# An attention and two-expert block on one core: gating and summing the last tiles elsewhere, TensorE products without a reader, and a third buffer of rows to be sorted

## The reference, cut to what matters

```python
mod = (silu(c) @ wmod).reshape(16, 6, 1, 256)     # sa, ca, ga, sb, cb, gb
ga, gb = sign * maximum(abs(.), 0.25)
h = layernorm(x) * (1 + ca) + sa                  # x: 16 batches x 256 tokens x 256
x = x + ga * attention(h)                         # 16 heads of 16, causal, low-rank q and kv
h = layernorm(x) * (1 + cb) + sb
# each token goes to one of two experts, by argmax of h @ Wg.T
out0 = gelu(h @ W0a.T + b0a) @ W0b.T + b0b
out1 = relu(h @ W1a.T + b1a) @ W1b.T + b1b
x = x + gb * where(expert == 0, out0, out1)
```

## Time and profile before

| | us |
|---|---|
| median of 3 runs | 574.53 (572.4 to 578.16) |
| the profiled execution: its time | 571.48 |
| its span | 569.7 |
| mean granted TensorE clock | 0.917 |
| busy: PE, PEld, DVE, ACT, POOL | 459.9, 364.0, 431.3, 293.4, 213.2 |

### The profile page before, as it was taken

One profiled execution on the slowest core, in us unless ns is written; L12 is line 12 of the kernel. 1 busy time (PEld: TensorE's weight loads), 2 busy tenths in 40 slices (PEclk: granted clock), 3 DMA queues, 4 the chain that ended last, 5 costly groups with the idle time before them and its releaser, 6 DMA issues.

```text
span 569.7 us, 11638 instructions
## 1 busy us (share of the span) xinstructions
PE 459.9 (81%) x4137; PEld 364.0 (64%) x4137; DVE 431.3 (76%) x987; ACT 293.4 (51%) x425; POOL 213.2 (37%) x233
## 2 busy tenths in 40 slices
PE   5627589889889889899889998898407999999950
PEld 4325467668668667667666777566306988888850
DVE  3657547798898898998888997785622799999960
ACT  1253157456466465465464674356204777677630
POOL 8422022323343343343242353213330044455475
PEclk9957679999999999999999999899656999999995
DMA  8596596596897898898899787723359514470111
GB/s 259 180 120 85 74 133 86 101 151 77 165 143 157 164 136 165 169 134 170 165 112 186 151 116 156 159 99 108 96 188 355 197 37 149 160 281 5 38 55 55
DMA packets 58793, 78.87 MB, mean 138 GB/s; under 512 B 6880, under 2 KB 47457, under 8 KB 58737
## 3 DMA queue, kind: packets, MB, share of 16 engines
q1 hardware_dynamic: 53632, 60.94, 57.9%
q0 software_dynamic: 4288, 16.80, 7.7%
q10 hardware_dynamic: 816, 0.39, 0.3%
HBM read 34.12 MB, written 18.96 MB: 93 GB/s over the span
## 4 chain that ended last, share of the span: by engine, by line
PE 35%; issue 27%; POOL 14%; DVE 10%; DMA 9%; ACT 2%; SPq 2%; POOLq 1%; ACTq 0%; DVEq 0%
DMA sorted_scratch<-comb,pos 5%; POOL out L1461 5%; PE ps_s L463 5%; PE ps_t L489 5%; POOL tile_rows L1454 5%; PE ps_o L506 4%; PE ps_s L443 3%; PE ps_t L443 3%; DVE mx L1110 2%; PE ps_o L507 1%; DVE z L988 1%; PE ps_c L410 1%; SPq L318 1%; DMA ks<-parts_k 1%; PE ps_a L524 1%
## 5 line engine op out<-in xcount | busy, mean ns | idle before, releaser
L1110 DVE TENSOR_REDUCE mx<-ps_s 128x2 f32<-128x512 f32 (+1 forms) x192 | 123.7, 684 | 38.6 <-PE ps_s L443 37.5
L867 ACT ACTIVATE p_all<-ps_t 128x1024 f32<-128x1024 f32 x93 | 95.1, 1023 | 98.4 <-PE ps_t L443 97.8
L463 PE MATMUL ps_s<-ks,qs 96*128 96x256 bf16 (+1 forms) x512 | 74.5, 255 | 37.2 <-issue 28.6
L463 PEld LDWEIGHTS ps_s<-ks,qs 96*128 96x128 bf16 x512 | 40.0, 101 | 54.1 <-issue 41.2
L489 PE MATMUL ps_t<-qs,ks 99*128 99x128 bf16 (+1 forms) x496 | 58.3, 251 | 4.6 <-DMA qs<-mx_rows 3.6
L443 PE MATMUL ps_s<-future_b,ident_b 128*128 128x256 bf16 (+1 forms) x192 | 61.8, 322 | 0.0
L1363 POOL TENSOR_TENSOR comb<-z,xs 128x512 f32<-128x512 f32 x16 | 20.4, 1276 | 102.8 <-DMA sorted_scratch<-comb,pos 62.2
L1454 POOL TENSOR_TENSOR tile_rows<-tile_rows 128x512 f32<-128x512 f32 x18 | 26.2, 1456 | 64.6 <-DVE tile_rows L1295 64.5
L489 PEld LDWEIGHTS ps_t<-qs,ks 99*128 99x128 bf16 x496 | 38.5, 99 | 15.0 <-issue 5.4
L1351 POOL TENSOR_TENSOR ln_rs<-ln_ve,neg_half 128x2 f32<-128x2 f32 x32 | 22.7, 711 | 66.8 <-DVE ln_ve L967 66.6
L410 PE MATMUL ps_s<-down_w,hid_hi 128*128 128x256 f32 x144 | 41.5, 288 | 4.6 <-DVE hid_lo L1275 4.6
(11 more groups left out here) (208 smaller groups left out, 1229.0 us busy)
## 6 DMA issues: line engine op xcount, KB each, us to landing
qs<-parts_q SPq DMA_DIRECT2D x96, 128.0 KB
ks<-parts_k SPq DMA_DIRECT2D x96, 128.0 KB
tile_rows<-sorted_scratch SPq DMA_DIRECT2D x9, 1026.0 KB, 9.7
rows<-mod_rows_scratch SPq DMA_DIRECT2D x16, 384.0 KB, 4.2
tile_rows<-sorted_scratch SPq DMA_DIRECT2D x9, 512.0 KB, 6.6
xs<-x SPq DMA_DIRECT2D x16, 256.0 KB, 6.0
comb<-mod_rows_scratch SPq DMA_DIRECT2D x32, 128.0 KB, 4.8
sorted_scratch<-wa SPq DMA_DIRECT2D x1, 1026.0 KB, 7.6
```

Source lines behind the costliest of these rows:

```text
L463: pe.matmul(ps_s[:, n * width:(n + 1) * width], qs[b.third][0:R, h, tile * P:(tile + 1) * P], ks[b.third][0:R, h, 0:width], start=n % a_ba ...
L867: act.activation((p0, p1)[tile][:, h0:h0 + n, :], scores_t(b, c)[:].rearrange("p (h s) -> p h s", h=n), ACT.Exp, scale=SCALE).then_inc(exp ...
L1110: dve.tensor_reduce(mx[:, tile, h0:h0 + n], ps_s[:, 512 * bank:512 * (bank + 1)].rearrange("p (h k) -> p h k", h=n), AX_X, ALU.max).then_i ...
```

## The change

There are three parts.

1. `comb`, `pos` and the semaphores `last_in` and `put` go from two buffers to three (index `b.third`, turns counted by `b.round`); the same four waits are now for the scatter of three batches before.
2. After the product that counts the first expert's rows (L687), TensorE makes 36 products of 512 bf16 columns into one half of `ps_s`. Nothing reads them. They wait for nothing, and `turn_tile(0)` stands behind them.
3. In the last turn of VectorE's loop (i = 8) the two `gate` operations of tile 7 stand right behind its `add_bias`, ahead of `hidden(8, 0)`, and no longer near the end of the turn. For tile 8 VectorE itself adds x1 after the gate, two more operations of 128x512, and GpSimd leaves out its two `finish_half`, so that `put_half` waits for VectorE's `last_ready`.

```diff
-        self.turn = n // 2
+        self.turn, self.round = n // 2, n // 3
-        pos = [sb(f"pos{i}", [P, TT], I32) for i in range(2)]
+        pos = [sb(f"pos{i}", [P, TT], I32) for i in range(3)]
-        comb = [early(f"comb{i}", [P, TT, ROW]) for i in range(2)]
+        comb = [early(f"comb{i}", [P, TT, ROW]) for i in range(3)]
+        WARM = 36
...
@@ SyncE, load_last_gate; place, add_attn and number_rows in the same way
-                wait(sp, put[b.pair], 32 * b.turn)
+                wait(sp, put[b.third], 32 * b.round)
...
-            for n in range(2):
-                sp.wait_ge(put[n], 16 * NB)
+            for n in range(3):
+                sp.wait_ge(put[n], 32 * ((NB - n + 2) // 3))
...
@@ TensorE
+            for n in range(WARM):
+                pe.matmul(ps_s[:, 512:1024], ident_b[:], future_b[:].unsqueeze(1).to_broadcast([P, 4, P]), start=True, stop=True)
             turn_tile(0)
...
@@ VectorE
             for i in range(NT):
                 add_bias(i - 1, 0)
                 add_bias(i - 1, 1)
+                if i == NT - 1:
+                    gate(i - 1, 0)
+                    gate(i - 1, 1)
                 hidden(i, 0)
...
-                gate(i - 1, 0)
-                gate(i - 1, 1)
+                if i < NT - 1:
+                    gate(i - 1, 0)
+                    gate(i - 1, 1)
                 target_rows(i)
             for q in range(2):
+                some = half_rows(NT - 1, q)
                 add_bias(NT - 1, q)
                 gate(NT - 1, q)
+                dve.wait_ge(y_gated, 2 * NT - 1 + q)
+                dve.tensor_tensor(some[:, :, 0:D], some[:, :, 0:D], some[:, :, D:2 * D], ALU.add).then_inc(last_ready, 1)
...
@@ GpSimd, put_half
-                pool.wait_ge(out_ready, 2 * i + q + 1)
+                if i < NT - 1:
+                    pool.wait_ge(out_ready, 2 * i + q + 1)
+                else:
+                    pool.wait_ge(last_ready, q + 1)
...
                 for q in range(2):
-                    finish_half(i, q)
+                    if i < NT - 1:
+                        finish_half(i, q)
                     put_half(i, q)
```

More of the change, by code:

```diff
@@ L223, in block_kernel @@
             "up_done gelu_done hid_ready hid_hi_ready hid_lo_ready down_part down_done".split())
[L224 removed]
+        y_ready, y_gated, out_ready, last_ready, row_of_ready = (sem(n) for n in "y_ready y_gated out_ready last_ready row_of_ready".split())
         g_in, rest_in, out_stored = ([sem(f"{n}{i}") for i in range(TILES)] for n in ("g_in", "rest_in", "out_stored"))
[L226 removed]
+        x_in, rows_in = (x_in0, x_in1), (rows_in0, rows_in1)
+        last_in, put = ([sem(f"{n}{i}") for i in range(3)] for n in ("last_in", "sorted"))
         q_in, k_in = (q_in0, q_in1), (k_in0, k_in1)
@@ L978, in second_stats @@
                     return
-                stats(b, 1, comb[b.pair][:, :, D:2 * D], x1_ready, b.n + 1)
+                stats(b, 1, comb[b.third][:, :, D:2 * D], x1_ready, b.n + 1)
             def normalise(b):
@@ L1036, in place @@
                 dve.wait_ge(offset_ready, b.n + 1)
-                wait(dve, put[b.pair], 32 * b.turn)
-                dve.tensor_tensor(pos[b.pair][:], BANK["RANK"][:, 0:TT], offset[:], ALU.add).then_inc(pos_ready, 1)
+                wait(dve, put[b.third], 32 * b.round)
+                dve.tensor_tensor(pos[b.third][:], BANK["RANK"][:, 0:TT], offset[:], ALU.add).then_inc(pos_ready, 1)
             def low_parts(some):
@@ L1357, in add_attn @@
                 pool.wait_ge(gated_ready, b.n + 1)
-                wait(pool, put[b.pair], 32 * b.turn)
+                wait(pool, put[b.third], 32 * b.round)
                 if b.n < 2:
@@ L1362, in add_attn @@
                 wait_alone(pool)
-                pool.tensor_tensor(comb[b.pair][:, :, D:2 * D], gated[:], xs[:, slots_of(b), :], ALU.add).then_inc(x1_ready, 1)
+                pool.tensor_tensor(comb[b.third][:, :, D:2 * D], gated[:], xs[:, slots_of(b), :], ALU.add).then_inc(x1_ready, 1)
             def number_rows(b):
@@ L1381, in put_rows @@
                 pool.wait_ge(number_ready, b.n + 1)
-                pool.wait_ge(last_in[b.pair], 32 * (b.turn + 1))
+                pool.wait_ge(last_in[b.third], 32 * (b.round + 1))
                 pool.wait_ge(x1_ready, b.n + 1)
                 for t in range(TT):
-                    pool.indirect_dma_start(sorted_dram, bass.IndirectOffsetOnAxis(ap=pos[b.pair][:, t:t + 1], axis=0),
-                                            comb[b.pair][:, t, :], None).then_inc(put[b.pair], 16)
+                    pool.indirect_dma_start(sorted_dram, bass.IndirectOffsetOnAxis(ap=pos[b.third][:, t:t + 1], axis=0),
+                                            comb[b.third][:, t, :], None).then_inc(put[b.third], 16)
             def h_low(b):
```

20 lines of the change are left out of this document (10 added, 10 removed).

## The result

The changed kernel took 580.50 us, median of 7 (577.84 to 583.40), against 576.04, median of 7 (572.40 to 578.16), for the kernel before. The ratio is 1.0089, 95% interval 1.0051 to 1.0127: slower by about 5 us, where I had forecast 6 us faster. The profiled execution of the changed kernel took 583.40 us with a span of 580.9, 11.2 more than the span before. That execution was the slowest of its seven, and the profiled one of before (571.48) was faster than all of its seven, so the two traces differ by 11 us where the medians differ by 4.5.

The account below looks back on a forecast made before the run. Usual first-stage steps were taken as bound by a ring of TensorE, SyncE's twelve issues and the transfers. End 3.6, products 0.9 and buffers 1.5 made 6.0 us off 574.53: 568.5 us, range 563.5 to 572.5.

Parts of the forecast that it names:

- The rival "slower": First-stage steps: VectorE running ahead lengthens TensorE's idle and the clock falls; up to 11 us slower, 585.6; chance 0.06.
- three buffers: First-stage steps: usual ones gain 0 as the stack's landing stays; two long ones give most of 1.5 us gained.
- The end: Last tiles: GpSimd loses two additions and the pauses behind them, gaining 3.6 us, bound 4.2; moved gates count 0.
- the pessimistic working: Last tiles: VectorE, with moved gates and two sums, is done by 557.1, before GpSimd reaches tile 8 at 557.57.
- The 36 products: Before the first tile: 10.8 us hidden under the load; faster transposes gain 0.9 us, 2.8 if the clock holds.
- 5.24 us after the work on the first tile had begun: First tile: when full clock returned; applied to the 36 products, it makes 12 slow and 24 fast.
- The rival that it holds: First tile: full clock lasts through the gap into up(0), giving 2.8 instead of 0.9 us, 566.6; chance 0.25.
- At most 8.9 of the 62.2 us reached another engine: First stage: of GpSimd's add_attn waits for scatters, only VectorE's 8.9 us wait was seen behind them.
- steps under 21 us: Sign in the changed profile that VectorE or GpSimd bounds the steps and the buffers are worth more than forecast.
- the buffers give nothing: First stage: the ring of stacks bounds every step, or earlier loads take the gain back; 570.0 to 572.0; chance 0.18.

Follow-up runs that it names:

- e1: Kernel before with only the third buffers of comb and pos, old end, without the 36 products: 587.39 us, ratio 1.0196.
- e3_wait_kept: Kernel before with only the third buffers, but add_attn still waits for the scatter of two batches before: 585.24 us, ratio 1.0167.
- e2: Kernel before with the new end and the 36 products, still two buffers: 571.01 us, ratio 0.9913.
- e12: Changed kernel plus 32 unused bytes behind pos and 10 unread products between the first tile's turning and its first products: 544.65 us, ratio 0.9467.
- e6: Changed kernel plus 32 unused bytes a partition behind the third pos, putting the stacks at a multiple of 256: 545.00 us, ratio 0.9443.
- e11: Changed kernel plus 160 unused bytes behind pos, putting the stacks 128 beyond a multiple of 256: 571.32 us, ratio 0.9926.
- e13: Kernel before plus 32 unused bytes behind the stacks, which stay while x, parts, rows and comb move: 576.33 us, ratio 1.0002.
- e15: Kernel before with the stacks moved 64 bytes to a multiple of 256 and everything behind them moved 512: 570.55 us, ratio 0.9905.
- e9: Kernel before plus 64 unused bytes behind pos, putting the stacks at a multiple of 256: 570.09 us, ratio 0.9903.
- e10: Kernel before plus 64 unused bytes behind pos, the new end and the 36 products, still two buffers: 563.38 us, ratio 0.9779.

## Why the prediction was wrong

**The sign and the size.** The forecast was 568.5 us with a range of 563.5 to 572.5; the result, 580.5, is outside on the other side. The rival that is slower had 0.06 of the chances. (The ratio of 1.0089 still lies within the 1% either way that had 0.43.)

**The step that failed** is the one on three buffers: "In usual steps what is late next is the landing of the stack, which doesn't move: 0." I had found the right bound, and took it as fixed. The landing moved by 0.25 us on average (15.74 to 15.99), because the new `pos` moved the stacks by 32 bytes. The idle of 1.5 to 2.1 us ahead of a step became 2.0 to 3.1, and the clock fell in eight of the twelve steps compared, not one. The term was +1.5 us with a lower bound of -2; alone it measured -11 (e1). In the early steps the idle grew by just what the landing did. Later it grew by some 0.5 us, and where the other half of that comes from stays open; e3_wait_kept has idles as long, so it isn't the scatter's wait.

**The rival "slower"** had the mechanism and its price: more idle at the start of a step, a fall of the clock, 1.95 us a fall (measured 1.8), up to 11 us. It had the wrong cause, VectorE running ahead, and I gave it 0.06 because that cause is weak. It is: e3_wait_kept takes it away and the falls stay. That it named the right sign is luck: the way to it was another. The rows that should have raised its chance whatever the cause were in the prediction: idles of 1.82 and 2.55 us with a fall behind them and of 2.14 without. Where nearly every step has such an idle, any of them may lose the clock; here landings a quarter of a us later went with falls in eight steps of twelve.

**The end** was worked out as 3.6 with a bound of 4.2. GpSimd's stretch is 4.2 us shorter in all, but that is no meeting of the bound. Tiles 7 and 8, which the sum is about, give 3.4: two issues took 1.36 and 1.00 beside VectorE's work, for 0.99 and 0.97, and the first addition 0.2 less. Another 0.8 come in tile 6, where issues of 1.41 and 1.37 us shrank to 0.97; the prediction had allowed 0.4 for one of them and counted 0. e2 has this part and the 36 products together at 5.0. VectorE's second sum was ready 0.43 us ahead of the first issue for tile 8, where the pessimistic working had left 0.47; but only the first sum is wanted by then, and it was 2.5 us early.

**The 36 products** gave 0.87 where 0.94 were worked out for the transposes, and the load landed 0.3 us later. They took 10.12 us where 10.8 were worked out. The "5.24 us after the work on the first tile had begun" counts from the first product; the transposes had begun 4.54 us earlier. The clock fell again in the standing for the split, as forecast. The rival that it holds (1.9 us more) was not this kernel; with the gap filled (e12) it is worth 1.7.

**The third buffers in themselves.** "At most 8.9 of the 62.2 us reached another engine" was right for this ring. It is a statement about the ring: with the stacks at a multiple of 256 the same wait decides, and the buffers are worth 19 us. The sign "steps under 21 us" for buffers that are worth more came in e6 (20.23). At the longer ring the buffers gave nothing (e11 against e2), which is the rival "the buffers give nothing": 570.0 to 572.0 us were forecast for it, and e11 took 571.32.

The best version by ratio, e6_aligned, is the changed kernel and one unused line: 545.0 us, ratio 0.9443, against 1.0089 without that line.

## What to carry to other kernels

An edit that allocates anything moves what is allocated behind it; ask which DMA destinations lie there, and look at the packets' durations before and after. Where transfers into SBUF bound a loop, try their destinations at multiples of 256 bytes in a partition before judging any other change. Here 32 bytes more made the changed kernel 6.4% faster, and the third buffers, which gained nothing elsewhere, gained 3.4% there. And where TensorE stands 2 us in each turn, count the clock as part of the loop: a few tenths of a us more of idle went with falls in eight turns of twelve, at 1.8 us each.

## What the runs showed of the hardware

- A DMA packet of 1024 bytes from SBUF to SBUF, on SyncE's queue, took 116 to 122 ns where it is written to a multiple of 256 bytes in the partition, 133 to 136 ns 128 or 192 beyond one, 140 to 145 ns 224 beyond (medians of 17 traces). The place that it is read from made no such difference (e13, e15).
- An int32 array of 2 elements a partition took 32 bytes of it, and moved all that was allocated behind it by as much.
- The clock fell to 1.2 GHz behind idles of 1.7 to 3.9 us at the start of a step, mostly when TensorE was at work again, and held behind others of up to 2.5 us. In e2, e9, e10, e13 and e15 it also fell around single idles of 1.2 to 2.6 us in the middle of a step. In e6, with idles of at most 1.1 at the starts, it never fell in a step.
- GpSimd paused 0.80 us between an addition and an indirect DMA of its result, and 0.30 between two indirect DMAs.
